# A seven-stage kernel whose per-stage semaphores are counted from zero, cleared by the sync engine one stage later, and whose statistics move into the stages' own programs

## The reference, cut to what matters

```python
x = _layernorm(x + _L0_attn_ref(x, ...))    # stage a: gated cumulative attention
x = _layernorm(x + _L0_xattn_ref(x, ...))   # stage b: cross attention, 16 heads, 77 context rows
x = _layernorm(x + _L0_ffn_ref(x, ...))     # stages m, e: router, shared experts, 8 routed experts
x = _layernorm(x + _L1_attn_ref(x, ...))    # stage s: selective scan
x = _layernorm(x + _L1_xattn_ref(x, ...))   # stage c: second cross attention
x = _layernorm(x + _L1_ffn_ref(x, ...))     # stage q: quantised feed-forward
```

## Time and profile before

| what | value |
|---|---|
| time, median of 3 runs | 2847.98 us |
| time, lowest and highest | 2846.27 and 2854.24 us |
| span of the profiled execution, first to last instruction | 2842.9 us |
| the same below the median of the runs | 5.1 us |
| mean granted TensorE clock | 0.933 |
| busy: PE, DVE, POOL, ACT | 87%, 80%, 72%, 60% |
| instructions | 43587 |

### The profile page before, as it was taken

One profiled execution on the slowest core, in us unless ns is written; L12 is line 12 of the kernel. 1 busy time (PEld: TensorE's weight loads), 2 busy tenths in 40 slices (PEclk: granted clock), 3 DMA queues, 4 the chain that ended last, 5 costly groups with the idle time before them and its releaser, 6 DMA issues. The chain is left out here.

```text
span 2842.9 us, 43587 instructions
## 1 busy us (share of the span) xinstructions
PE 2473.1 (87%) x13058; PEld 1470.2 (52%) x13058; DVE 2260.3 (80%) x3693; ACT 1704.9 (60%) x3383; POOL 2044.5 (72%) x1817
## 2 busy tenths in 40 slices
PE   7969999989979966898989989899989999995665
PEld 5646666656646642333433333333358878873222
DVE  5879999756634449999999999999857777776887
ACT  7847787744312326667676676776555565654665
POOL 5529999757746655999999999999636666664554
PEclk9969999989989988999999999999999999997555
DMA  5911111001145535555455454555523332320000
GB/s 166 422 57 23 24 23 24 8 29 42 43 114 161 160 102 186 184 184 189 178 181 187 176 194 169 196 187 189 185 79 89 90 85 86 88 81 27 19 18 23
DMA packets 238423, 331.81 MB, mean 117 GB/s; under 512 B 46433, under 2 KB 186998, under 8 KB 217346
## 3 DMA queue, kind: packets, MB, share of 16 engines
q1 hardware_dynamic: 227538, 311.48, 33.1%
q0 software_dynamic: 9088, 16.94, 1.7%
q10 hardware_dynamic: 1584, 0.79, 0.1%
HBM read 231.45 MB, written 99.50 MB: 116 GB/s over the span
## 5 line engine op out<-in xcount | busy, mean ns | idle before, releaser
L1875 POOL TENSOR_TENSOR s_drive<-s_du,s_b_sb 128x1024 f32<-128x1024 f32 x256 | 600.6, 2360 | 40.2 <-DVE s_state_ps L2242 40.1
L2242 DVE TENSOR_TENSOR_SCAN s_state_ps<-s_decay_ps,s_drive 128x512 f32<-128x512 f32 x416 | 487.1, 1216 | 43.4 <-ACT s_decay_ps L2028 34.5
L2390 PE MATMUL s_y_ps<-s_read,w_ident 128*128 128x512 f32 x832 | 405.6, 613 | 90.6 <-DVE s_read L2255 90.4
L2028 ACT ACTIVATE s_decay_ps<-s_delta,neg_rate 128x508 f32<-128x508 f32 x512 | 340.6, 682 | 151.3 <-DVE s_state_ps L2242 93.4
L2390 PEld LDWEIGHTS s_y_ps<-s_read,w_ident 128*128 128x128 f32 x832 | 149.0, 191 | 323.0 <-DVE s_read L2255 186.5
L2255 DVE TENSOR_TENSOR s_read<-s_state_ps,s_c_sb 128x1024 f32<-128x1024 f32 x208 | 254.5, 1224 | 7.2
L1421 POOL DMA_INDIRECT m_y_scratch<-e_y,e_index x156 | 152.8, 979 | 93.5 <-DVE e_y L1467 51.7
L2679 POOL TENSOR_TENSOR c_share<-c_p,c_norm 128x1232 f32<-128x1232 f32 x64 | 148.6, 2322 | 83.2 <-DVE c_norm L2811 83.2
L742 ACT ACTIVATE b_pT<-b_turn_ps 77x512 f32<-77x512 f32 x256 | 144.5, 592 | 74.2 <-PE b_turn_ps L871 74.2
L2879 PE MATMUL c_f_ps<-c_ctxT,w_c_wqk 128*128 128x308 f32 x512 | 179.0, 438 | 8.1 <-DMA c_ctxT<-in_ctxT_dram 5.2
L1045 POOL DMA_INDIRECT m_rows_scratch<-m_xs,m_index x128 | 128.4, 1003 | 60.4 <-issue 39.8
(11 more groups left out here) (389 smaller groups left out, 6203.4 us busy)
## 6 DMA issues: line engine op xcount, KB each, us to landing
s_b_sb<-s_bc_scratch SPq DMA_DIRECT2D x64, 1024.0 KB, 6.3
s_c_sb<-s_bc_scratch SPq DMA_DIRECT2D x64, 1024.0 KB, 5.4
c_vp_scratch<-s_stage SPq DMA_DIRECT2D x152, 256.0 KB, 2.3
c_vp<-c_vp_scratch SPq DMA_DIRECT2D x64, 576.0 KB, 4.1
m_rows_scratch<-fill SPq DMA_DIRECT2D x33, 1040.0 KB, 26.8
e_w<-in_m_we_dram SPq DMA_DIRECT2D x39, 384.0 KB, 3.2
e_xg<-m_rows_scratch SPq DMA_DIRECT2D x39, 260.0 KB, 3.4
s_read<-m_y_scratch SPq DMA_DIRECT2D x32, 256.0 KB, 3.1
```

Of the source, the lines that this page charges most:

```text
L1875: nc.gpsimd.tensor_tensor(drive[:, (g * states + n) % drives, :, :], du[:, s, :, :], b_sb[:, n, :].unsqueeze(1).broadcast_to([128, halves, ...
L2028: nc.scalar.activation(decay[:, m, :, 1:], delta[:, s, m, :].rearrange("p (b t) -> p b t", t=T)[:, :, 1:], ACT.Exp, scale=core.neg_rate[:, ...
L2242: nc.vector.tensor_tensor_scan(home[:, h, :], decay[:, h, :, :].rearrange("p b t -> p (b t)"), drive[:, (g * states + n) % drives, h, :], ...
L2390: last = nc.tensor.matmul(y_ps[:, m, :], core.ident[:, :], read[:, r % deep, m, :], start=False, stop=False)
```

## The change

The count of every semaphore starts at 0, so `open_signals` goes, with its block. A wait for "0 so far" on a fresh semaphore is left out, or asked only from the second round on. `close_signals` goes too: `Core` keeps the signals of this stage (`own`) and of the one before (`spent`), and SP clears the spent ones in the stage after theirs, as the last thing of its program (in m, as the only thing). The scatters' ten semaphores are kept for the whole kernel and never cleared. The waits for weights move from the head of a stage to the end of SP's program in the stage before. `finish_statistics` is no block any more: DVE does it at the end of its program in a, b and c, behind one more wait for the last `bn_stats` (for which a and c get a semaphore `measured`), and ACT's square root stands at the end of ACT's program. Its three small tiles are allocated once.

```diff
 class Signal:
-    def __init__(self, sem, per_pass=1, first=1):
+    def __init__(self, sem, per_pass):
     def at(self, done, k):
-        return done * self.per_pass + k + self.first
+        return done * self.per_pass + k

-def open_signals(nc, signals, landed):
...
-            for weights in landed:
-                sp.wait_ge(weights.sem, weights.value)
-            for signal in signals:
-                sp.sem_inc(signal.sem, 1)
-def close_signals(nc, signals):
...
-            for signal in signals:
-                nc.gpsimd.sem_clear(signal.sem)
+def clear_spent(core, sp):
+    for signal in core.spent:
+        sp.sem_clear(signal.sem)

 class Core:
+    def next_signals(self):
+        self.spent_ctx.close()
+        self.spent, self.spent_ctx = self.own, self.own_ctx
+        self.own, self.own_ctx = [], ExitStack()
+    def lasting(self, name, per_pass):
+        return Signal(self.ctx.enter_context(self.nc.semaphore(name)), per_pass)
+    def sig(self, name, per_pass=1):
+        self.own.append(Signal(self.own_ctx.enter_context(self.nc.semaphore(name)), per_pass))
+        return self.own[-1]

+def root_of_spread(core, act, name):
+    done = "abc".index(name)
+    act.wait_ge(core.folded, 8 * done + 4)
+    core.nc.scalar.activation(core.stat_root[:, :], core.rstd[:, :], ACT.Sqrt).then_inc(core.rooted, 1)

-def finish_statistics(core, name):
+def finish_statistics(core, dve, name):
...
-        block = ctx.enter_context(nc.Block())
...

 def phase_aft(core):
-        open_signals(nc, signals, [])
-        ctx.callback(close_signals, nc, signals)
         block = ctx.enter_context(nc.Block())
...
+            clear_spent(core, sp)
+            sp.wait_ge(core.landed["b"].sem, core.landed["b"].value)
...
             over_periods(step)
+            root_of_spread(core, act, "a")
...
-                    nc.vector.bn_stats(core.stats[:, g * GB + j, :], x[:, g * GB + j, :])
+                    last = nc.vector.bn_stats(core.stats[:, g * GB + j, :], x[:, g * GB + j, :])
+                last.then_inc(measured.sem, 1)
...
             over_periods(step)
+            dve.wait_ge(measured.sem, measured.at(NG - 1, 1))
+            finish_statistics(core, dve, "a")

 def phase_cross0(core):
-        open_signals(nc, signals, [core.landed["b"]])
-        ctx.callback(close_signals, nc, signals)
...
             def load(i, s):
-                sp.wait_ge(loaded.sem, loaded.at(i, 0))
+                if behind(i, 1):
+                    sp.wait_ge(loaded.sem, loaded.at(i, 0))
...
             for i in range(B):
                 load(i, i % slots)
+            clear_spent(core, sp)
+            sp.wait_ge(core.landed["m"].sem, core.landed["m"].value)
+            sp.wait_ge(core.filled.sem, core.filled.value)
...
+            dve.wait_ge(x_steps.sem, x_steps.at(B - 1, 2))
+            finish_statistics(core, dve, "b")

 def route_and_share(core, table):
-        open_signals(nc, signals, [core.landed["m"], core.filled])
-        ctx.callback(close_signals, nc, signals + landings)
         block = ctx.enter_context(nc.Block())
+        @block.sync
+        def _(sp):
+            clear_spent(core, sp)

 def run_experts(core, table, y_dram):
-        open_signals(nc, signals, [])
-        ctx.callback(close_signals, nc, signals + landings)
...
+            clear_spent(core, sp)
+            sp.wait_ge(core.landed["s"].sem, core.landed["s"].value)
+            sp.wait_ge(core.landed["c"].sem, core.landed["c"].value)

 def phase_scan(core):
-        open_signals(nc, signals, [core.landed["s"], core.landed["c"]])
...
             store_lots(NG, 1, states)
+            clear_spent(core, sp)

 def phase_cross1(core):
-        open_signals(nc, signals, [core.landed["c"]])
...
+            clear_spent(core, sp)
+            sp.wait_ge(core.landed["q"].sem, core.landed["q"].value)
...
-                nc.vector.bn_stats(core.stats[:, i, :], x[:, i, :])
+                nc.vector.bn_stats(core.stats[:, i, :], x[:, i, :]).then_inc(measured.sem, 1)
...
+            dve.wait_ge(measured.sem, measured.at(B - 1, 1))
+            finish_statistics(core, dve, "c")

 def phase_quantised(core):
-        open_signals(nc, signals, [core.landed["q"]])
```

More of the change, by code:

```diff
@@ new lines, in finish_statistics @@
+    done = "abc".index(name)
+    folded = core.folded
+    gap, root, turn = core.stat_gap, core.stat_root, core.stat_turn
+    mean_even, spread_even = core.stats[:, :, 1], core.stats[:, :, 2]
+    mean_odd, spread_odd = core.stats[:, :, 4], core.stats[:, :, 5]
+    nc.vector.tensor_tensor(gap[:, :], mean_even, mean_odd, ALU.subtract)
+    nc.vector.tensor_tensor(core.rstd[:, :], spread_even, spread_odd, ALU.add).then_inc(folded, 1)
+    nc.vector.tensor_tensor(core.mean[:, :], mean_even, mean_odd, ALU.add)
@@ L165, in phase_aft @@
+    dve.wait_ge(folded, 8 * done + 7)
+    nc.vector.scalar_tensor_tensor(core.rstd[:, :], turn[:, :], 1.5, root[:, :],
+                                   ALU.add, ALU.mult).then_inc(folded, 1)
 def phase_aft(core):
@@ L1008, in route_and_share @@
         place_steps = sig("m_place_steps", 4)
-        scattered = [from_zero(f"m_scattered{n}", 16 * top_k * GB) for n in range(slots)]
+        scattered = [core.lasting(f"m_scattered{n}", 16 * top_k * GB) for n in range(slots)]
         up_ready = sig("m_up_ready", shared_units)
@@ L1381, in run_experts @@
         y_ready = sig("e_y_ready")
-        scattered = [from_zero(f"e_scattered{n}", 16 * GB) for n in range(y_slots)]
+        scattered = [core.lasting(f"e_scattered{n}", 16 * GB) for n in range(y_slots)]
         def landed(eng, slots, t):
@@ L1552, in ps @@
             return ctx.enter_context(nc.psum_tensor(name, shape, dt))
-        signals = []
+        core.next_signals()
         def sig(name, per_pass=1):
-            signals.append(Signal(ctx.enter_context(nc.semaphore(name)), per_pass))
-            return signals[-1]
+            return core.sig(name, per_pass)
         tap_w = core.w["s_taps"]
@@ L1590, in phase_scan @@
         f0_ps, f1_ps = f_ps[:, 0, :], f_ps[:, 1, :]
-        gap = sb("s_first_gap", [128, B])
-        root = sb("s_first_root", [128, B])
+        gap, root = core.stat_gap, core.stat_root
         batches = (range(0, 1), range(1, 3), range(3, NG))
@@ L3402, in build @@
             setup(core)
[L3403 to L3404 removed]
+            phase_aft(core)
+            phase_cross0(core)
             phase_moe(core)
```

125 lines of the change are left out of this document (48 added, 77 removed).

## The result

The changed kernel takes 2828.2 us (median of 4 runs, 2823.8 to 2834.5), the one before took 2849.8 beside it (4 runs, 2846.3 to 2854.2): 0.9929 of its time, with a 95% interval of 0.9917 to 0.994. The profiled execution took 2823.8 us, with a span of 2821.8 where it had been 2842.9.

The account below looks back on a forecast made before the run. No engine was taken as the bound; semaphore work between stages was. Additions 12.9, clears 6.6 and block ends 3.9, less 0.3 us, give 23.1 us off the 2848.0 median: 2824.9 us, range 2817 to 2833.

Parts of the forecast that it names:

- The model of a change of block: Between stages: 0.059 us per SP addition, 0.065 per POOL clear, 0.28 per block end; 12.9, 6.6 and 3.9 us saved.
- The seven places: Savings at setup to a 2.2, a-b 4.3, b-m 3.5, m-e 3.1, e-s 6.2, s-c 1.8, c-q 2.3 us.
- The start: Setup to a: ACT's first table load starts near 3.3 us, x already there, saving 2.2 us; bounds 0 and 2.3.
- The statistics: Behind a, b and c: length kept, ACT's table load covered, DVE's new wait costing 0.1 us three times, 0.3 us.
- Code is late: Rival at stage heads: without block cover first instructions wait for code, 14 us given back, 2839 us; chance 0.06.
- the one row without cover: Change from c to its statistics, without SP or POOL semaphore work: 0.30 us, cited against late code.
- Not the semaphores: Rival between stages: the stretches are waits that stay, only 14 block ends go, 3.9 us, 2844 us; chance 0.03.
- dear clears: Rival at the ends of s and c: SP's clears cost up to 0.6 us each and outrun their cover, 2856 us; chance 0.02.
- The clock moves: Rival at c's head (0.8 us) and in q (2 us a return, 8 us either way): 2817 or 2833 us; chance 0.11.

Follow-up runs that it names:

- the repetition: The changed kernel, unaltered, timed and profiled once more against the kernel before: 2829.0 us, 0.993 of before.
- statistics in blocks: Changed kernel with the statistics behind a, b and c put back in a block of their own: 2825.4 us in one run.
- opens back: Changed kernel with counts starting at 1 and SP's additions back in a block ahead of each stage: 2840.8 us, 0.9971 of before.
- clears x8: Changed kernel with every semaphore clear on SP issued eight times in a row: 2846.7 us, 0.9994 of before.
- the one with more matmuls: Changed kernel with q's first product of 512 columns issued three times in place of once: 2824.6 us, 0.9917 of before.
- the second profile of before: The kernel before, unchanged, run and profiled a second time: 2848.1 us, span 2846.2, q 248.7 us against 245.4.
- closes back: Changed kernel with POOL's clears back in a block of their own behind a, b, m and e: 2831.0 us, 0.9946 of before.
- spare blocks: Changed kernel with four nearly empty blocks, one SP addition in each, ahead of each of the seven stages: 2837.7 us, 0.9963 of before.

## Why the prediction was right, and where it was not

The forecast was 2824.9 us, in a range of 2817 to 2833; the median is 2828.2, and 2829.0 in the repetition. Faster by over 0.3% had 0.94, and is what came.

- *The model of a change of block* held in each of its prices. Additions of 0.059 us: the opens put back cost 15.4 us where the model said 14.9. Clears on POOL of 0.065: 6.8 against 7.1. Block ends of 0.28: 0.28 to 0.30 with the statistics in blocks, and 0.33 to 0.35 with an addition. SP's clear had no row and was taken at 0.065; it is 0.060. The seven places came out within 0.1 us each, but for m to e at 0.2, and the sum at 23.18 against 23.1.
- *The start* was put at 2.2 and gave 2.13: x was there, as worked out from the queue's 0.40 MB.
- *The statistics.* DVE's wait was put at 0.1 us three times, and costs 0; the table load was covered, as its place in ACT's program said.
- *Code is late* (2839) did not happen: DVE starts b, m, c and q 0.32 or 0.33 us behind its last operation, next to 0.30 in the one row without cover, and the gaps ahead of a, e and s came out within 0.2 us of the model. Its price was read wrongly: the earlier trace rows is not the longest wait of its kind, since POOL stood up to 4.7 us on "issue" at line 1045 of the kernel before; by that the rival would have been 33 us, more than the change saves (waits of POOL before: us in total, times, longest us):

```profile
POOL m_rows_scratch L1045 <- issue: 39.8, 113, 4.7
```

- *Not the semaphores* (2844) and *dear clears* (2856) fell with opens back and clears x8.
- *The clock moves.* At the head of c nothing was gained: PE's idle time fell from 4.97 to 3.49 us, not to 3.2, and the clock fell all the same (the timeline of PE, then windows with the columns of the earlier trace rows):

```profile
2045.87 3.96 PE L2879 MATMUL c_f_ps<-c_ctxT,w_c_wqk 128*128 128x308 f32 x8 [3.49 <-DMA c_ctxT<-in_ctxT_dram]
```

```profile
2046.00:2048.00 2.00, 2.00 (x4) 1.11 (x5) 1.43 (x10) 0.52 (x1) 1.92 (x5) 0.50 0.91 330
...
2050.00:2054.00 4.00, 3.63 (x12) 1.77 (x12) 0.00 (x0) 2.74 (x6) 0.00 (x0) 1.00 0.00 0
```

- *The step that failed* is my reading of the earlier trace rows, that a round of q is 12 us or 14 by the clock, and "a return is worth up to 2 us". The round of 12 us is the last one in which POOL has no result to finish yet; it took 12.0 to 12.2 us in every kernel but the one with more matmuls, at one clock or the other. And with half of the time at full clock the rounds still took 14.4. What moves q by most of its 5 us is which of DVE and POOL comes first: the scaling was caught 6 to 14 times in 16 rounds, at 0.84 us each. The size that I gave the rival (8 us either way) covered it, by a wrong mechanism.
- *The term that was mis-sized is the stages, taken as fixed.* The forecast came from the median, 2848.0 less 23.1, and the gaps gave 23.2; by medians the change was worth 21.6, 19.3 and 18.2 us. Two profiles of before differ by 3.3 us in q alone, and of the changed kind by 3.6 in b, 4.1 in s, 2.6 in q. The 2.1 us that the stages gave back in the first pair of profiles, and the 3.3 us by which the median missed the forecast, are no more than such differences, and that the range held them is in part luck. But one part of it came with the changed kernel in both its profiles: its long rounds of q are 0.14 us longer, which over q I estimate at 1.5 us or so.
- *The span of the earlier trace rows was a short one.* Every timed execution here lies 1.7 to 2.2 us above its span, so the profiled one of before took about 2845 us, less than any of the four timed beside it. This bears on the forecast of the span (2819.8, measured 2821.8), not on that of the time.

**What stays open.** Of q's 251.0 and 250.4 us in two runs of the changed kernel I account for all but about 2 us against the second profile of before, which had as many scalings caught. Its long rounds were 14.49 us and the changed kernel's 14.63; 0.11 of this stands as idle "issue" time of DVE ahead of L3271 in every round (0.28 against 0.17 us), for which the profile names no cause. It is not the numbers that are waited for: closes back, statistics in blocks and spare blocks wait in q for the same numbers as the changed kernel and show 0.17 there, with rounds of 14.50 to 14.53; opens back waits for the numbers of before, shows 0.27 one step earlier, ahead of `q_x_back`, and has rounds of 14.63. In a round of the changed kernel, of closes back and of opens back:

```profile
2709.31 0.61 DVE L3271 SCALAR_TENSOR_TENSOR x<-q_o_ps,q_h_back,x 128x128 f32 x2 [0.28 <-issue]
```

```profile
2715.51 0.61 DVE L3286 SCALAR_TENSOR_TENSOR x<-q_o_ps,q_h_back,x 128x128 f32 x2 [0.17 <-issue]
```

```profile
2726.37 0.17 DVE L3241 TENSOR_TENSOR q_x_back<-q_x_top,q_w_mean 128x8 f32<-128x8 f32 x1 [0.27 <-issue]
```

The place of the code is one thing that is left; nothing tests it. One thing said of the kernel ahead is wrong here: q is not unrolled. Its groups 2 to 13 are one loop of the program (`eng.Fori(2, NG - 2)`, line 3041 of the kernel before), so these rounds run the same instructions again and a fixed delay in them counts each time. Nor is it told apart how much of s's first part is the clock's effect and how much the clock's cause.

## What to carry to other kernels

Semaphore work in a block of its own cost about 0.06 us an instruction with every other engine standing, and 0.28 us or a little more for the block; over seven stages that was 23 us. Put clears on a queue that waits anyway, and look how long it waits there (here 1.6 us at the tightest). And before a stage's few us are ascribed to a change or to the clock, profile the old kernel a second time: four of seven stages here have two outcomes or more. In q and near the end of s they go by which of two engines, or of an engine and a transfer, comes first; in a and b they go with the stretches at half clock. One wait that fixed the order in q shortened it by 10.4 us, about half of what the whole change saved.

## What the runs showed of the hardware that was not expected

- An instruction of VectorE on 2 columns took 1.00 us instead of 0.16 where a product of 512 columns had begun on GpSimd 0.1 us before it; one on 512 columns took 1.26 instead of 0.43 where such a product had begun 0.06 us before it.
- Adding a wait on GpSimd made the kernel 13.8 us faster (2825.1 to 2811.3), 10.4 of it in the profiles' q.
- A clear costs the same on SyncE (0.060 us) as an addition there (0.059), and about what GpSimd's costs (0.065).
- Raising TensorE's granted clock in q from about 0.54 to 0.76 was worth 0.2 us in a round of 14.6: that the clock stood at half did not tell what bounds this stage.
- A gap of 3.49 us on TensorE at the head of c was followed by half clock, as one of 4.97 had been.
